# One core, a two-layer transformer program: the cached keys of its paged attention turned by VectorE in place of TensorE, and its pages copied in DRAM and loaded plainly in place of gathers

## The reference, cut to what matters

```python
    def _L1_cond2_ref(x, Wq, Wk, Wv, Wo, q_norm_w, k_norm_w, k_cache, v_cache, block_table, cache_seqlens):
        ...
        q = _rope(_rmsnorm(q, q_norm_w), pos)
        k = _rope(_rmsnorm(k, k_norm_w), pos)
        L = NPP * PSIZE                                   # 16 pages x 32 tokens = 512
        kc = k_cache[block_table].reshape(bsz, L, HK, D)  # cache: 64 pages x 32 tokens x 8 heads x 128
        vc = v_cache[block_table].reshape(bsz, L, HK, D)
        k_all = jnp.concatenate([kc, k], axis=1)          # 512 cached + 128 own keys
        v_all = jnp.concatenate([vc, v], axis=1)
        ...
        scores = jnp.einsum('bqhd,bkhd->bhqk', q, k_all) * SCALE
        probs = jax.nn.softmax(jnp.where(valid, scores, -1e+30), axis=-1)
        o = jnp.einsum('bhqk,bkhd->bqhd', probs, v_all).reshape(bsz, seqlen, HQ * D)
        return jnp.einsum('bse,de->bsd', o, Wo)
...
    x = x + _L1_attn_ref(_L1_cond_ref(x, ...), ...)       # attention 1
    x = x + _L1_ffn_ref(_L1_cond2_ref(x, ...), ...)       # attention 2, quantised FFN
```

## Time and profile before

| what | us |
| --- | --- |
| three runs, median | 2049.22 (2048.26 to 2049.91) |
| span of the profiled execution | 2048.5 |
| PE busy in it | 1990.9 (97%) |
| DVE busy | 1534.9 (75%) |
| ACT busy | 1332.9 (65%) |
| POOL busy | 808.5 (39%) |

### The profile page before, as it was taken

The page is one execution under the profiler, slowest core; times in us unless marked ns, Lnnn a source line. Parts: engine busy times, 40 slices in busy tenths (PEclk is TensorE's granted clock), DMA queues, the critical chain, the costliest instruction groups (busy, mean ns, idle before and its releaser), DMA issues.

```text
span 2048.5 us, 35844 instructions
## 1 busy us (share of the span) xinstructions
PE 1990.9 (97%) x12449; PEld 1697.2 (83%) x12456; DVE 1534.9 (75%) x3385; ACT 1332.9 (65%) x3810; POOL 808.5 (39%) x800
## 2 busy tenths in 40 slices
PE   6999999999999999999999999999999999999985
PEld 5777777888888888888888888888888888888873
DVE  5777764556666555687887888878878888788997
ACT  4676763445554544566776777767767777677785
POOL 3200015100000000056666666666666666666653
PEclk9999999999999999999999999999999999999998
DMA  7211101101201110121111111211111112112000
GB/s 259 93 33 47 53 1 73 62 32 37 68 32 45 49 53 1 58 78 32 62 52 31 62 52 31 83 31 59 55 31 62 53 32 64 51 32 83 27 32 31
DMA packets 45010, 108.60 MB, mean 53 GB/s; under 512 B 15634, under 2 KB 21010, under 8 KB 40354
## 3 DMA queue, kind: packets, MB, share of 16 engines
q1 hardware_dynamic: 28450, 72.74, 10.2%
q0 software_dynamic: 16384, 33.59, 5.5%
HBM read 103.14 MB, written 3.15 MB: 52 GB/s over the span
## 4 chain that ended last, share of the span: by engine, by line
PE 90%; DVE 5%; ACT 3%; issue 1%; DMA 1%; SPq 0%; DVEq 0%; ACTq 0%
PE PS L1662 10%; PE PS L1487 9%; PE PS L1430 9%; PE PS L1674 8%; PE PS L1566 8%; PE PS L1629 7%; PE PS L1647 7%; PE PS L1580 4%; PE PS L1443 4%; PE PS L1632 3%; PE PS L342 3%; PE PS L1458 3%; PE PS L1473 2%; PE PS L498 1%; PE PS L1465 1%; PE PS L1589 1%
## 5 line engine op out<-in xcount | busy, mean ns | idle before, releaser
L2527 POOL DMA_INDIRECT kcache<-in_kcache,rows x256 | 251.5, 982 | 533.1 <-DVE x_res L1818 462.4
L2535 POOL DMA_INDIRECT vcache<-in_vcache,rows x256 | 257.4, 1005 | 124.2 <-issue 58.4
L1991 DVE CUSTOM_DVE_ANT_0 pr<-PS,ffn_weights,sm 128x640 f32<-128x640 f32 x256 | 224.6, 885 | 89.5 <-PE PS L1632 89.5
L2007 DVE TENSOR_TENSOR prT_lo<-PS,prT_hi 128x512 fp32r<-128x512 f32 x320 | 209.1, 685 | 44.8 <-ACT prT_hi L2384 41.1
L2373 ACT ACTIVATE pr<-pr,sm 128x640 f32<-128x640 f32 x256 | 212.3, 831 | 39.9 <-DVE sm L1991 39.6
L2384 ACT ACTIVATE prT_hi<-PS 128x512 fp32r<-128x512 f32 x320 | 179.1, 597 | 72.3 <-PE PS L1647 62.0
L1647 PE MATMUL PS<-consts,pr 128*128 128x128 f32 x1280 | 174.0, 273 | 2.7 <-DVE prT_lo L2007 1.6
L1647 PEld LDWEIGHTS PS<-consts,pr 128*128 128x128 f32 x1280 | 149.7, 141 | 28.7 <-issue 3.6
L2541 POOL TENSOR_TENSOR vcached_lo<-vcache,vcached_hi 128x512 fp32r<-128x512 f32 x64 | 83.3, 1301 | 225.4 <-ACT vcached_hi L2356 225.4
L1629 PE MATMUL PS<-kT_hi,qT_hi 128*128 128x320 f32 x512 | 154.4, 309 | 1.8 <-DVE sm L1991 1.3
L1629 PE MATMUL PS<-kT_lo,qT_hi 128*128 128x320 f32 x512 | 154.1, 309 | 0.0
(11 more groups left out here) (323 smaller groups left out, 6186.6 us busy)
## 6 DMA issues: line engine op xcount, KB each, us to landing
arena<-in_wqkv SPq DMA_DIRECT2D x16, 1536.0 KB, 6.5
arena<-in_wo SPq DMA_DIRECT2D x16, 1024.0 KB, 5.3
arena<-in_wcT SPq DMA_DIRECT2D x8, 1024.0 KB, 6.6
kcache<-in_kcache,rows POOLq DMA_INDIRECT x256
vcache<-in_vcache,rows POOLq DMA_INDIRECT x256
arena<-in_xT SPq DMA_DIRECT2D x8, 256.0 KB, 7.5
x_res<-in_x SPq DMA_DIRECT2D x1, 2048.0 KB, 13.2
ffn_weights<-in_alibi SPq DMA_DIRECT2D x2, 1024.0 KB, 6.9
```

The lines of the kernel that those rows point to most:

```text
L1991: dve.tensor_tensor_reduce(pr2[:, h, :].rearrange("p (a n) -> p a n", a=2), PS[:, SCORE_BANK[h]:SCORE_BANK[h] + 2, 0:HALF], keymask[:, b, ...
L2007: dve.tensor_tensor(prT2[1][:, n % 3, :, :].rearrange("p h n -> p (h n)"), bank(4 + n % 2), prT2[0][:, n % 3, :, :].rearrange("p h n -> p ...
L2527: pool.indirect_dma_start(out=kcache[:, c, :], out_offset=None, in_=T["kcache"], in_offset=bass.IndirectOffsetOnAxis(ap=rows[:, g, b, c:c ...
L2535: pool.indirect_dma_start(out=vcache[:, c, :], out_offset=None, in_=T["vcache"], in_offset=bass.IndirectOffsetOnAxis(ap=rows[:, g, b, c:c ...
```

## The change

PE's turn_cached_k, POOL's load_keys and load_values, the tables of row numbers (dve_positions and a part of pool_tables) and DVE's lo_of_cached_k go. In their place:

- gather(b) on SP, in attention 1 in the loop over groups: for each of the 16 pages of sequence b, SP reads the page's number from SBUF into a register and issues two DRAM-to-DRAM copies of the whole page (32 tokens × 8 heads × 128 × 4 bytes = 131 KB each), of keys and of values, into kpages and vpages. In all 8 × 32 copies.
- load_keys(n) and load_values(n) are SP loads from these copies. Keys come in four DMAs of 32 partitions, each of pieces of 32 numbers (128 bytes), 2048 pieces an item, so that turning each 32x32 block by itself gives the whole transpose; values come in one DMA of 512-byte pieces.
- turn_cached_k(n) is one DVE instruction from SBUF to SBUF, 128x512. hi_of_cached_k on ACT reads its result from SBUF, and lo_of_cached_k is a POOL instruction.
- SP's loads for attention 2 are written into one order with its weight loads; in the last items the FFN's loads stand among them.

```diff
+            def gather(b):
+                for s in range(SLOTS):
+                    n = (s % 4) * B * CHUNKS + b * CHUNKS + s // 4
+                    page = sp.value_load(page_ids[0:1, n:n + 1], min_val=0, max_val=NPAGE - 1)
+                    sp.dma_start(kpages[b, s:s + 1].rearrange("a t g d -> a (t g d)").rearrange("a (r n) -> a r n", r=32),
+                                 T["kcache"].rearrange("(a r) d -> a r d", a=NPAGE)[bass.ds(page, 1), :, :].rearrange("a (t g) d -> a t (g d)", t=PAGE)
+                                 ).then_inc(s_gathered, 16)
+                    sp.dma_start(vpages[b, s:s + 1].rearrange("a t g d -> a (t g d)").rearrange("a (r n) -> a r n", r=32),
...
+            def load_keys(n):
+                g, b = group_of(n)
...
+                wait(sp, a2_kcT, n)
+                for j in range(4):
+                    sp.dma_start(kraw[j * PAGE:(j + 1) * PAGE, :].rearrange("t (s d) -> t s d", s=SLOTS),
+                                 kpages[b, :, :, g, j * PAGE:(j + 1) * PAGE].rearrange("s t d -> t s d")).then_inc(a2_kg, 16)
+
+            def load_values(n):
+                g, b = group_of(n)
...
+                wait(sp, a2_vcl, n)
+                sp.dma_start(vcache[:], vpages[b, :, :, g, :].rearrange("(c s) t d -> (s t) c d", c=CHUNKS)
+                             ).then_inc(a2_vg, 16)
...
@@ -1341,6 +1370,7 @@
                 if g == 0:
                     sp.wait_ge(s_x2, B)
                     table(1)
+                gather(g)
                 if 3 <= g < 7:
                     keep_units(2 * g - 6)
                 if 2 <= g < 6:
...
+            load_qkv_weights2(0)
+            load_out_weights2(0)
+            sp.wait_ge(s_gathered, 16 * 2 * B * SLOTS)
+            load_keys(0)
+            load_qkv_weights2(1)
+            load_values(0)
+            load_keys(1)
+            for i in range(LAST):
+                load_values(i + 1)
+                load_keys(i + 2)
+                g, b = group_of(i)
+                if b == 0:
+                    load_out_weights2(g + 1)
+                if b == B - 1 and g + 2 < G:
+                    load_qkv_weights2(g + 2)
...
@@ -1679,7 +1715,6 @@
                 scores(i)
                 if i + 1 < ITEMS:
                     project_kv(i + 1)
-                    turn_cached_k(i + 1)
                 if i >= 1:
                     project_out(i - 1)
...
-            def lo_of_cached_k(n):
-                dve.wait_ge(a2_kch, n + 1)
-                dve.tensor_tensor(kT2[1][:, 0:CACHED], bank(3), kT2[0][:, 0:CACHED], ALU.subtract).then_inc(a2_kcl, 1)
+            def turn_cached_k(n):
+                dve.wait_ge(a2_kg, 16 * 4 * (n + 1))
+                wait(dve, a2_kcl, n)
+                dve.transpose(kcache[:], kraw).then_inc(a2_kcT, 1)
...
@@ -2034,6 +2070,8 @@
                     row_max(i, h)
                 if i:
                     lo_of_o(i - 1)
+                if more:
+                    turn_cached_k(i + 1)
                 reciprocals(i, (0, 1))
                 normalise(i, 0)
                 normalise(i, 1)
@@ -2049,7 +2087,6 @@
                     add1(ITEMS - 1)
                 if more:
                     lo_of_own_v(i + 1)
-                    lo_of_cached_k(i + 1)
                     norm_k(i + 1)
```

More of the change, by code:

```diff
@@ L35 @@
 QKV = (GH + 2) * HD
-PAGE, SLOTS = 32, 16
+PAGE, SLOTS, NPAGE = 32, 16, 64
 CACHED = PAGE * SLOTS
@@ L158, in build @@
         halves = sb("pool_constants", [P, 24])
[L159 to L162, removed]
+        page_ids = sb("page_ids", [1, B * SLOTS], I32)
         clen_i, clen = sb("clen_i", [P, B], I32), sb("clen", [P, B])
@@ L1166, in sp_paged_inputs @@
         def sp_paged_inputs(sp):
-            for q in range(4):
-                sp.dma_start(page_i[q * 32:(q + 1) * 32, :], T["pages"][q, :].partition_broadcast(32)).then_inc(s_setup, 16)
+            sp.dma_start(page_ids[:], T["pages"].rearrange("q n -> (q n)").unsqueeze(0)).then_inc(s_setup, 16)
             sp.dma_start(clen_i[:], T["cache_len"].partition_broadcast(P)).then_inc(s_setup, 16)
@@ L1331, in sp_attentions, with load_out_weights2 @@
+            def load_out_weights2(g):
+                wait(sp, a2_wol, GH * g)
+                sp.dma_start(stage_out.rearrange("p h n -> p (h n)"),
+                             T["wo2"][g, :, :, :].rearrange("p h n -> p (h n)")).then_inc(a2_wo, 16)
             sp.wait_ge(s_prec, 3)
+            sp.wait_ge(s_setup, 16 * NSETUP)
             table(0)
@@ L1369, in sp_attentions @@
                 sp.dma_start(brow[:, w, :], T[bias].partition_broadcast(P)).then_inc(s_fi, 16)
+            for i in range(LAST + 1, ITEMS - 1):
+                load_values(i + 1)
+                if i + 2 < ITEMS:
+                    load_keys(i + 2)
         wT16 = area(0, KT * D).bitcast(BF16).rearrange("p (w t n) -> p w t n", w=2, t=KT)
@@ L1582, in project_kv @@
                 mm.then_inc(a2_kv, 1)
-            def turn_cached_k(n):
-                pe.wait_ge(a2_kg, 16 * CHUNKS * (n + 1))
-                if n == 0:
-                    pe.wait_ge(a1_kTc, ITEMS)
-                for c in range(CHUNKS):
-                    mm = pe.transpose(bank(3, P, c * P), kcache[:, c, :], ident)
-                mm.then_inc(a2_kcT, 1)
             def turn_q(n):
@@ L1614, in scores @@
                             pe.wait_ge(a1_max, ITEMS)
+                    if h == 1 and i == 0:
+                        pe.wait_ge(a1_kTc, ITEMS)
                     if h == 2 and i == 0:
@@ L1722, in turn_hidden @@
                 pe.wait_ge(s_hq, n + 1)
-                if i is not None and i + 1 < ITEMS:
-                    pe.wait_ge(a2_kcl, i + 2)
+                if i is not None:
+                    pe.wait_ge(a2_max, 4 * i + 2)
                 else:
@@ L2360, in hi_of_cached_k @@
                 act.wait_ge(a2_kcT, n + 1)
-                act.activation(kT2[0][:, 0:CACHED], bank(3), ACT.Copy).then_inc(a2_kch, 1)
+                wait(act, a2_sc, 4 * n)
+                act.activation(kT2[0][:, 0:CACHED], kcache[:], ACT.Copy).then_inc(a2_kch, 1)
             def hi_of_q(n):
@@ L2521, in pool_paged, with lo_of_cached_k @@
             ch = Chain(pool, s_chp, counted["pool"])
-            def load_keys(n):
-                g, b = group_of(n)
-                wait(pool, a2_kcT, n)
-                for c in range(CHUNKS):
-                    pool.indirect_dma_start(out=kcache[:, c, :], out_offset=None, in_=T["kcache"],
-                                            in_offset=bass.IndirectOffsetOnAxis(ap=rows[:, g, b, c:c + 1], axis=0)
-                                            ).then_inc(a2_kg, 16)
-            def load_values(n, cs=range(CHUNKS)):
-                g, b = group_of(n)
-                wait(pool, a2_vcl, n)
-                for c in cs:
-                    pool.indirect_dma_start(out=vcache[:, c, :], out_offset=None, in_=T["vcache"],
-                                            in_offset=bass.IndirectOffsetOnAxis(ap=rows[:, g, b, c:c + 1], axis=0)
-                                            ).then_inc(a2_vg, 16)
+            def lo_of_cached_k(n):
+                pool.wait_ge(a2_kch, n + 1)
+                pool.tensor_tensor(kT2[1][:, 0:CACHED], kcache[:], kT2[0][:, 0:CACHED], ALU.subtract).then_inc(a2_kcl, 1)
             def lo_of_cached_v(n):
```

61 lines of the change are left out of this document (26 added, 35 removed).

## The result

The changed kernel takes 2213.52 us, the median of 4 runs (2211.5 to 2213.91), beside 2048.74 us before (4 runs); the ratio is 1.08, 95% interval [1.0787, 1.0813]. Its profiled execution has a span of 2211.8 us, 163.3 more than before, and took 2213.9 us as a run. Of the runs further down, one execution of the kernel with one transpose, 2793 us long at a mean granted clock of 0.654 in place of 0.995, is left out of its median.

What follows compares the result with a forecast made beforehand. PE was taken to bound the kernel, busy throughout both attention stages. The sum 2048.5 + 0 + 25 + 118 + 10 = 2201.5 us of span, plus 0.7 for the runs' median, gave 2202 us; range 2130 to 2285.

Steps and rivals of the forecast that it cites:

- Part 1: PE in attention 2: the four transposes of cached keys leave; 0 to 0.07 us an item, counted as nothing.
- Part 2: DVE in attention 2: the transpose delays the softmax chain by 0.40 us an item, +25 us, ends +7 and +64.
- T: Price of DVE's transpose in attention 2: taken as 0.60 us, 0.32 from below and 1.23 from above.
- Part 3: POOL in attention 2: loses eight gathers, gains a subtraction that lies beside PE's work; nothing.
- Part 4: SP in attention 1: page copies make later loads late, five PE stalls of 17.0, 24.1 and 3 × 25.5, 118 us.
- 5 Bt − 18.4: Attention 1: total of PE's stalls in us, Bt being SP's time for a batch of 16 pages, taken as 27.2.
- Part 5: PE's clock behind the stalls of attention 1: granted lower, 2 us each, +10 us; from nothing to 43.
- Part 6: Small loads and positions of layer 0, loads at the start of attention 2: put at 0, between −1 and +6.
- A: Attention 1: the copies' traffic, not SP, sets the pace, 39 us a batch; 2261 us, chance 0.14.
- B: Attention 2: key loads in 128-byte pieces don't land within an item, 22.4 us an item; 2481 us, chance 0.07.
- C: Attention 2: the transpose is hidden on DVE and PE keeps its 22 us; 2155 us, chance 0.12.
- D: Attention 1: SP is quick, about 0.25 us a page, stalls shrink to 8 us; 2035 us, chance 0.05.

Runs made afterwards that it cites:

- the kernel with one transpose: Kernel before with one of PE's four transposes of cached keys in each item of attention 2 in place of four: 2048.72 us, ratio 0.9998.
- the small copies: Changed kernel, batches in their place on SP, each copy moving 4 KB of its 131 KB page and attention 2 loading from the cache itself: 2210.12 us.
- the fastest version: Changed kernel with the copy batches later on SP, and on DVE the transpose first and lo_of_o ahead of the row maxima: 2027.64 us, ratio to before 0.9898.

## Why the prediction was right, step by step

**Part 1** (four transposes leave PE, gain nothing): shown. The kernel before with three of them gone takes the same time, the changed kernel's project_out waits for oT_lo in 64 items, and only an earlier oT_lo brings the gain out.

**Part 2** (the transpose in front of the softmax chain, +25 us for 62 items): the wait is shown, 25 us remained when the stalls were gone (2074.21 against 2048.95 us in that comparison), and 33 left with the transpose moved away. That the sum came out so near is in part luck, for its terms were off both ways. T came out at 0.62 for 0.60 from start to start, and ACT's normalisations start 0.63 us later. Most items grew by 0.53 us in place of 0.40. Of this the wait for ACT that the prediction named is some 0.36 (project_out to the first product of q: 1307.00 − 1302.96 = 4.04 us against 1109.80 − 1106.12 = 3.68), so the slack was nearer 0.27 than 0.20; the other 0.17 are the wait for prT_lo, which the prediction did not have. Against that the seven longer items of before vanished and took 4.4 us off (their excess over 17.17: 0.78, 0.44, 0.77, 0.43, 0.80, 0.77, 0.43). The Trainium skill's rate for the transposing front-end (Vector Engine (DVE) Microarchitecture Reference, section 3.8) gave my estimate of 0.53 us plus a fixed part; the measured 0.62 us agrees.

**Part 3** (POOL's new work is hidden, nothing) did not hold in the changed kernel, as far as its rows show. POOL's subtraction lies beside PE's work as the prediction said, but it stretches the last instruction of rotate_k on DVE by 0.7 us, right ahead of prT_lo. With the transpose moved away this is hidden (the wait for prT_lo is gone, and the subtraction back on DVE changes nothing that can be told); together with the transpose it gives the 0.17 us, some 10 us in all. This price is an estimate from the rows: no run takes POOL's subtraction out and leaves the transpose where the change put it.

**Part 4** (SP's batches, five stalls, 118 us): shown, 125.8 us. The stalls are the five that were named, ended by the waits that were named. The term that was mis-sized is the page: 1.88 us against 1.70, since the two issues took 0.60 and 0.53 in place of 0.45 and 0.51; the register load was 0.75 against 0.74. With a batch of 16 × 1.88 = 30.1 us the formula 5 Bt − 18.4 gives 132; that is 6 more than measured. The rows of the units landed faster than assumed: 453.49 − 449.17 = 4.3 us from the first issue to DVE's start, and 3.3 us in the median from issue to landing, where the median before was 5.3. Rows that land 1 to 2 us sooner, four times, are about the difference.

**Part 5** (the clock, +10): 12.7 us are left when the gaps are taken from the 138.5. Behind the five gaps PE works for 4.4 to 5.0 us at 0.50, which is 2.2 to 2.5 us lost each, some 12 together; the rest stays open. The value taken, 2 us each, was near it, and the upper bound of 43 far off.

**Part 6** (nothing in layer 0 and at the start of attention 2): no row speaks against it; the sum ahead of attention 2 is closed by the gaps and the clock to within 1 us.

In all the span is 10.3 us above the 2201.5 forecast: 8 of it from the stalls, 2.7 from the clock, and the rest nearly cancels.

The rivals: A fell by the small copies. B did not come up. Four issues of a key load take 1.90 us of SP's queue in an item (at 1303.55 of the changed kernel), and a load lands 2.3 us after its issue:

```profile
consts<-gathered_k_pages SPq DMA_DIRECT2D x256, 64.0 KB, 2.3
```

The Trainium skill's wish for pieces of 512 bytes (DMA: Bandwidth & Descriptors, Specifications) decides nothing here: some 4 us for 2048 pieces of 128 bytes lie far inside an item of 17.7. C was half right: the transpose can be hidden, but hiding it doesn't give PE's gain, as the run with the transpose first shows. Its own condition, an earlier lo_of_o, does give it: with the stalls gone as well that run is 21 us below the kernel before. D fell with the page's price, 1.88 us against its 0.25.

## What to carry to other kernels

An instruction train on an engine that only issues DMAs costs every load behind it in the order its full length, less the slack that this load had, however few bytes it moves; put it where the next load is due latest. Work taken from the busiest engine is won only if what it waits for next is early too: read when the next operand is ready before counting the saving. An extra instruction on another engine is free in front of that engine's longest wait and dear just behind it; here the same transpose cost 33 us behind the row maxima and nothing that shows ahead of them. Work handed to another engine is saved only if the two don't hold each other up: look for instructions that have become longer, and not only for those that are gone.

## What the runs showed of the hardware that was not expected

POOL can hold up DVE. In the changed kernel the last instruction of rotate_k, 128x128 from SBUF with two inputs, has a median of 1008 ns where it had 293 before:

```profile
L1996 DVE TENSOR_TENSOR qk<-qk,swapped x64: 292/1008/1015, 1028.2 to 2150.6; 128x128 f32<-128x128 f32 x64
```

In the fastest version it starts at 1103.48 and ends at 1104.54, just behind POOL's subtraction (1103.11 + 1.29 = 1104.40); with POOL moved, the instruction that then lies beside it is stretched instead, also until POOL's end (1107.27 + 1.28 = 1108.55; 1107.30 + 1.33 = 1108.63). The Trainium skill (SBUF — State Buffer, Terms) says that DVE and GpSimd arbitrate for a shared port pair, held for a whole instruction, and that the loser fully blocks; these rows agree.

An issue of 4 KB costs SP as much as one of 131 KB: in the run with small copies a page took 326.17 − 324.28 = 1.89 us of SP, beside 1.88.
